# When a shared DMA queue may issue the next stage's weights: two added waits, and two other PSUM banks for six products

## The reference, cut to what matters

```
hg = einsum('bnf,gf->bng', h3, Wg[:, :F])
qg = einsum('blf,gf->blg', q, Wg[:, F:]) + bg
attn = sigmoid(hg[:, :, None, :] + qg[:, None, :, :])
qi = einsum('bnlf,blf->bnf', attn, q)
alpha = sigmoid(einsum('bnf,gf->bng', h3, Wq[:, :F]) + einsum('bnf,gf->bng', qi, Wq[:, F:]) + bq)
hn = alpha * tanh(qi) + (1.0 - alpha) * h3
```

## Time and profile before

| | |
|---|---|
| median of 3 runs | 1323.51 us (1323.05 to 1326.19) |
| the profiled execution | 1323.78 us, span 1322.0 us |
| mean granted TensorE clock | 0.994 |
| PE busy | 1282.2 us, 97% of the span |
| DVE, ACT, POOL busy | 978.1, 784.2, 216.5 us |
| DMA | 195.35 MB, q1 busy for 43.6% of 16 engines' span |

### The profile page before, as it was taken

One profiled execution on the slowest core, in us unless ns is written; L12 is line 12 of the kernel. 1 busy time (PEld: TensorE's weight loads), 2 busy tenths in 40 slices (PEclk: granted clock), 3 DMA queues, 4 the chain that ended last, 5 costly groups with the idle time before them and its releaser, 6 DMA issues.

```text
span 1322.0 us, 24350 instructions
## 1 busy us (share of the span) xinstructions
PE 1282.2 (97%) x10110; PEld 1119.5 (85%) x10110; DVE 978.1 (74%) x1772; ACT 784.2 (59%) x1301; POOL 216.5 (16%) x108
## 2 busy tenths in 40 slices
PE   9999999999999989999999999999999999999998
PEld 8999644699844589889988999889999999998986
DVE  8775777865777788788788668867676777789555
ACT  3455898645698756566656565645455554547344
POOL 0210587300297500002121001010000000000100
PEclk9999999999999999999999999999999999998999
DMA  9276159136157334053365461534455555233200
GB/s 365 73 252 198 54 130 289 43 138 199 42 143 237 100 132 156 33 203 106 139 239 176 152 212 60 195 130 154 169 179 182 186 188 195 78 126 149 84 1 25
DMA packets 31121, 195.35 MB, mean 148 GB/s; under 512 B 4241, under 2 KB 4370, under 8 KB 15011
## 3 DMA queue, kind: packets, MB, share of 16 engines
q1 hardware_dynamic: 31010, 193.79, 43.6%
HBM read 183.55 MB, written 3.93 MB: 142 GB/s over the span
## 4 chain that ended last, share of the span: by engine, by line
PE 79%; DVE 9%; ACT 6%; DMA 4%; issue 1%; POOL 1%; SPq 0%; POOLq 0%; DVEq 0%; ACTq 0%
PE PS L370 65%; PE PS L1182 4%; DMA RT<-AS 3%; PE PS L1191 3%; PE PS L375 3%; ACT PS L1291 2%; PE PS L777 2%; DVE WK L1351 1%; DVE WL L313 1%; ACT WH L306 1%; PE PS L1604 1%; PE PS L552 1%; DVE SM L634 1%; ACT WK L1288 1%; ACT WK L2182 1%
## 5 line engine op out<-in xcount | busy, mean ns | idle before, releaser
L313 DVE TENSOR_TENSOR WL<-w,WH 128x768 fp32r<-128x768 f32 x366 | 351.9, 972 | 152.1 <-ACT WH L306 150.5
L306 ACT ACTIVATE WH<-w 128x768 fp32r<-128x768 f32 x381 | 315.6, 840 | 238.8 <-PE PS L370 232.2
L370 PE MATMUL PS<-XS,WH 128*128 128x256 f32 x2256 | 408.4, 284 | 2.4 <-DVE XS L584 1.4
L370 PEld LDWEIGHTS PS<-XS,WH 128*128 128x128 f32 x2256 | 347.8, 189 | 7.2 <-issue 2.8
L370 PE MATMUL PS<-XS,WL 128*128 128x256 f32 x1128 | 317.9, 282 | 0.0
L370 PEld LDWEIGHTS PS<-XS,WL 128*128 128x128 f32 x1128 | 213.1, 189 | 0.0
L1351 DVE TENSOR_TENSOR WK<-PS,WK 128x1024 f32<-128x1024 f32 x128 | 151.4, 1220 | 47.2 <-ACT PS L1291 43.2
L1433 POOL TENSOR_TENSOR WK<-WK 128x1024 f32<-128x1024 f32 x62 | 148.2, 2395 | 183.7 <-ACT WK L1288 183.6
L370 PE MATMUL PS<-WH,GS 128*128 128x256 f32 x864 | 159.9, 284 | 0.9 <-DVE GS L584 0.9
L1291 ACT ACTIVATE PS<-PS 128x1024 f32<-128x1024 f32 x130 | 125.6, 1008 | 26.8 <-PE PS L1182 26.8
L370 PEld LDWEIGHTS PS<-WH,GS 128*128 128x128 f32 x864 | 135.5, 190 | 2.7 <-DVE GS L584 1.4
(11 more groups left out here) (303 smaller groups left out, 2075.8 us busy)
## 6 DMA issues: line engine op xcount, KB each, us to landing
w<-f2W_in SPq DMA_DIRECT2D x40, 1152.0 KB, 5.4
w<-Wrel_in SPq DMA_DIRECT2D x12, 1152.0 KB, 7.1
WK<-qrep_in SPq DMA_DIRECT2D x16, 768.0 KB, 6.4
w<-f1Wi_in SPq DMA_DIRECT2D x8, 1152.0 KB, 6.1
w<-f1Wo_in SPq DMA_DIRECT2D x8, 1152.0 KB, 5.2
w<-f3Wqkv_in SPq DMA_DIRECT2D x6, 1152.0 KB, 15.3
RT<-qg_rows SPq DMA_DIRECT2D x16, 384.0 KB, 6.8
RT<-AS SPq DMA_DIRECT2D x32, 192.0 KB, 6.6
```

What stands on the lines that cost most here:

```text
L306: A.e.activation(w_hi(i), w_raw(i), ACT.Copy).then_inc(*hi("w", i))
L313: V.e.tensor_tensor(w_lo(i), w_raw(i), w_hi(i), ALU.subtract).then_inc(*lo("w", i))
L370: ins = T.e.matmul(o, l, r, start=i == 0 and first, stop=i == n - 1 and last, skip_group_check=lint)
```

## The change

At b = 5 and b = 6 SP no longer issues the two weight units right behind the block's rows, but first waits for that block's queries and rows to land. And the six key tiles go to the banks 7, 0, 4, 5, 4, 5 in place of 4, 5, 6, 7, 4, 5.

```diff
@@ gate_sync
                 queries(b)
                 rows_q(b)
                 rows_h(b)
-                if b == 5:
-                    load_units(nxt + 6)
-                if b == 6:
-                    load_units(nxt + 12)
+                if b in (5, 6):
+                    L.wait_ge(qin[b % 2], n, b)
+                    L.wait_ge(gin[b % 2], n, b)
+                    load_units(nxt + 6 if b == 5 else nxt + 12)
@@ l3ffn_pe
             pe_gemm_T("f3k", zk, 0, 6, xs_at, lambda f: (act, "f3k", f), None,
-                      lambda f: [(LB[:, 768 + f * P:768 + (f + 1) * P], adT)], (4, 5, 6, 7))
+                      lambda f: [(LB[:, 768 + f * P:768 + (f + 1) * P], adT)], (7, 0, 4, 5, 4, 5))
```

## The result

The changed kernel takes 1332.01 us (median of 9 runs, 1327.66 to 1337.69) against 1325.18 us for the kernel before, measured beside it (9 runs, 1320.15 to 1326.19). The ratio is 1.0056, 95% interval 1.0039 to 1.0073: 7.4 us slower. The forecast was 1325.6 us, 2.1 more than before and so within the 0.3% that can't be told from no change; the measured time lies above its range, which ended at 1329.0. The profiled execution, 1337.69 us, is the slowest of the nine. Of all runs in this text one, of 2482.76 us, is left out of the ratios (one of 12 of the spread variant with the old banks).

A forecast was written before the change was run, and what follows sets the result against it. PE, busy for 97% of the span, was taken to bound the kernel. The waits' +3.3 us and the banks' -1.2 us made +2.1 us on the median of 1323.51 us: 1325.6 us, range 1319.5 to 1329.0 us.

The forecast's parts named there:

- The first edit's term: Both gates: waits at b = 5 and 6 make block 7 start 1.6 and 1.7 us later, together +3.3 us.
- rows(5), now alone: 194.13 + 7.0: First gate: without weights behind, rows(5) land 7.0 us after issue, at 201.1; block 5 gains 1.05 us.
- The pair ... 8.3 us: Gates: two weight units land in 8.3 us, 5.4 for one alone and 2.9 for the second.
- rows(6) 5.7 us behind the weights: Gates: with nothing behind them, rows(6) land 5.7 us after W(5), 7.5 less 1.8; first gate 215.2 us.
- rows(7) 7.5 behind: Gates: with one unit still following, rows(7) land 7.5 us after W(6), at 231.1 us in the first gate.
- Ring order holds after all: Rival, both gates: weights behind rows slow nothing, rows(6) and (7) not relieved; +5.4 us, 1328.9 us, chance 0.06.
- two stalls go: Gates: blocks 5 and 6 start on time or nearly, while a longer stall appears at block 7.
- 12.78 us: Gates: time from block to block if nothing is late, 203.39 - 189.56 - 1.05.
- the most that the first edit can give back: Both gates: late rows cost 1.7 + 1.6 = 3.3 us in all in the kernel before.
- Slower: TensorE's clock falls at the stall before block 7: Rival, both gates: PE stands about 3 us, clock loss costs 1.7 us each; +5.5 us, 1329.0 us, chance 0.10.
- The banks, -1.2: Last layer's keys: first key tile follows at once in bank 7, wait of 1.33 us falls to about 0.1; -1.2 us.
- the waits do what one would hope: First rival, gates: rows(6) and (7) land in time, -3.3 - 1.2 = -4.5 us, 1319.0 us, chance 0.14.

The follow-up runs named there:

- spread variant with the old banks: Kernel before, with the four weight units issued one each behind the landings of rows(2) to rows(5), key tiles' banks unchanged: 1322.32 us, ratio 0.9984.
- waits alone: The changed kernel with its four waits but the old bank list (4, 5, 6, 7): 1332.93 us, ratio 1.0065 against the kernel before.
- two fills: The changed kernel with 18 or 7 idle matmuls on PE before block 7's first selection: 1334.15 and 1331.68 us.
- spread variant: The changed kernel with its four weight units issued one each behind the landings of rows(2) to rows(5), new banks: 1321.37 us, ratio 0.9979.
- wait at 6 alone: The changed kernel with the waits at b = 6 only, W(5) right behind rows(5), new banks: 1327.49 us, ratio 1.0019.
- one unit behind rows(7): The changed kernel with one of W(6)'s two units at b = 6 behind the landing, the other right behind rows(7): 1323.99 us, ratio 0.9995.
- first fill: The changed kernel with 18 idle matmuls on PE right before block 7's first selection: 1334.15 us, ratio 1.0081.
- wait at 5 alone: The changed kernel with the waits at b = 5 only, W(6) right behind rows(6), new banks: 1326.12 us, ratio 1.0018.
- short fill: The changed kernel with 7 idle matmuls on PE before block 7's first selection: 1331.68 us, ratio 1.0054.

## Why the prediction was wrong

The direction and the place of the loss were right: W(6) in front of rows(7) makes block 7 late. Two steps failed. The first edit's term, +3.3 us, was too small: it measured +9.3 in the profile, 6.5 by late rows and 2.9 by the clock, and +8.6 by the time of the waits alone. And the fall of the clock at block 7's stall, put at nothing in the sum and kept among the rivals, happened.

Its chain can be laid beside the trace, counted from the first issue of rows(5) (192.57 and 402.31 us forecast, 195.78 and 409.54 in the changed kernel). W(5)'s and W(6)'s second units landed after these times from their issue:

```profile
w<-Wroot_in SPq DMA_DIRECT2D x1, 1152.0 KB, 8.7
...
w<-Wrel_in SPq DMA_DIRECT2D x1, 1152.0 KB, 7.8
...
w<-f0Wq_in SPq DMA_DIRECT2D x1, 1152.0 KB, 7.7
...
w<-f0Wk_in SPq DMA_DIRECT2D x1, 1152.0 KB, 9.2
```

They were issued at 205.81, 220.76, 418.90 and 433.12 us.

| landed, us after rows(5)'s issue | forecast | gate 1 | gate 2 |
|---|---|---|---|
| rows(5) | 8.5, 8.6 | 9.6 | 9.0 |
| W(5) | 16.9, 17.0 | 18.7 | 17.1 |
| rows(6) | 22.6, 22.7 | 24.6 | 23.1 |
| W(6) | 31.0, 31.1 | 32.8 | 32.8 |
| rows(7) | 38.5, 38.6 | 39.6 | 40.7 |
| block 7's start, before | | 37.0 | 36.9 |

- *"rows(5), now alone: 194.13 + 7.0"*. The relief came, but to 8.1 and 7.4 us for the last transfer, not 7.0, which I had taken from a single block. Over the 14 landings of rows(5) without weights behind, in the seven kernels that wait at b = 5, it is 7.7 on average (6.3 to 8.6); over the six with weights behind, in three kernels that don't, 8.7 (8.1 to 9.6). So weights behind cost 1.0 us, not 1.8. Block 5's stall did go, as forecast.
- *"The pair ... 8.3 us"* measured 9.1, 8.2, 8.1 and 9.6 us from the first unit's issue.
- *rows(6) 5.7 us behind the weights*: 5.8 and 6.1. *rows(7) 7.5 behind*: 6.8 and 8.0. Both good. The rival *"Ring order holds after all"* wanted 7.5 for rows(6) too, and falls with the 5.8 and 6.1.
- *"two stalls go"*: one went. Block 6 had gaps of 2.52 and 1.12 us, where it had 1.06 and 1.97 before.
- Since each link starts when the one before has landed, the errors are handed on: up to 1.9 us in the first gate, of which 1.1 was left at rows(7), and 2.1 in the second. Block 7 came 2.6 and 3.9 us later than before, instead of 1.6 and 1.7. The range had allowed 3.1 for this, by varying the last links only, never the first. With the waits alone and the two fills there are six more gates with these four waits; there rows(7) let block 7 start 1.5 to 4.3 us later than before, and the mean of all eight is 2.6. So late rows cost an estimated 5.3 us in the two gates of an ordinary execution; with 3 for the clock and -1.2 for the banks that is +7.1, where +7.4 was measured.
- *"12.78 us"* from block to block was read with the 0.62 us gap of an ordinary step, but a block's first load has 0.76 before it even when nothing is late, and 12.9 is right. Late rows cost 2.5 us before, not 3.3, and *"the most that the first edit can give back"* was 0.8 us too high.
- *"Slower: TensorE's clock falls at the stall before block 7"*, 0.10, happened in both gates of the profiled run, at 1.4 to 1.5 us each (4.56 us for a step of 3.08). I had priced it at 1.7. By my own sum PE would stand "about 3 us" and the mark was guessed at 2.5: at this the clock's fall belonged into the forecast, and the two things are not independent, as the same late landing makes both.
- *The banks, -1.2*: right, 1.20 us by the trace. *No cost for keys 4 and 5*: right, no gap.
- *The first rival, "the waits do what one would hope"* needs rows and a pair of weights within one period, and they don't fit: 9.0 + 8.1 us, and then the next rows still have to come, against 12.9. With one unit, after 5.4 us, they nearly do, as the spread variant shows.

## What to carry to other kernels

A wait that holds prefetches back until an urgent transfer has landed doesn't shorten the queue; it moves them in front of the next urgent transfer, and leaves the DMA engines idle between (here a share of 0.00 to 0.11 for about 2 us). Before adding one, lay a whole period out: urgent transfer, landing, the held-back ones, and see that they are done before the next urgent issue; if they aren't, hold back less at a time, or issue earlier where the queue is idle. And in a chain where each link starts at the landing of the one before, take each link's duration from several rows, carry the errors along the whole chain, and price what a longer stall sets off (here the clock) with it.

## What the runs showed of the hardware

- The clock's fall doesn't follow the length of PE's gap alone. Gaps of 2.96 and 5.50 us (changed kernel), 3.11 (waits alone) and 4.12 us (wait at 6 alone) were followed by a stretch at 0.50; gaps of 2.94 (waits alone), 3.27 (one unit behind rows(7)) and 3.09 us (the first fill, before block 6) were not.
- After the data has all but stopped, a landing can still be late. In the second gate of the changed kernel the transfers took 0.53 of the engines in the last half microsecond before 449.0 us and 0.19 or less from there, yet rows(7) landed at 436.92 + 13.35 = 450.27.
- With no weights behind it, the last 192 KB of rows(5) took between 6.3 us (wait at 5 alone, first gate) and 8.6 us (the short fill, second gate) to land: 2.3 us of spread in the same place of the same program.
